# Two attention stages of a decoder kernel: the order of Norm's transposes, the second scores and the turned value products

## The chip, the cores and the metric

The kernel runs on one core of one Trainium2 chip. The metric is the device time of one launch in microseconds (us). The kernel before takes 1344.28 us, the median of 3 runs (1343.42 to 1345.02).

## The reference

A decoder of two layers over 32 sequences of 128 tokens with 256 features. Each layer adds three blocks to x, each on a LayerNorm of x:

```python
x = x + _L0_attn_ref(_layernorm(x), ...)         # 16 heads of 16, rotary factors on q and k
x = x + _L0_xattn_ref(_layernorm(x), ctx, ...)   # entangled cross attention, one head
x = x + _L0_ffn_ref(_layernorm(x), ...)          # routed experts with low-rank parts
x = x + _L1_attn_ref(_layernorm(x), ...)         # 16 heads of 16
x = x + _L1_xattn_ref(_layernorm(x), ctx, ctx, mask, ...)   # 16 heads, one mask row for all
x = x + _L1_ffn_ref(_layernorm(x), ...)          # ternary weights, inner LayerNorm
# a head: softmax(q k^T / 4) v; then the output projection
```

## The kernel before

The residual x stays in SBUF. Work goes by groups of two sequences (256 tokens), 16 groups a layer. `attention_stage` runs twice: once for the first block ("the first stage" below, with rotary factors, `rope`), and once for the fourth and fifth blocks together ("the second stage": 16 self groups, then 16 cross groups with a mask, `at(G)[0].cross`). Between them and behind them lie stages that the change doesn't touch.

Each engine has its own program, a function `group(G, parity)` made of `first_half` and `second_half`; the engines meet only through semaphores, so the order in which each function issues its steps is the order on that engine. A group G overlaps with three others: its Norm and projections are made while G-1 and G-2 are in their attention. Groups 3 to 10 of a layer are in a hardware loop, the others are unrolled, and the unrolled ones also carry pieces of preparing the next stage's weights.

For one sequence of a group (half a group) the steps are these.

- `maximum_scores` (TensorE, L1307): a cheap pass of q k^T, "first scores", in tiles of 32 rows, four heads' strips at a time, in four PSUM banks. It waits until the exponentials of three of the four banks of the sequence before are done. VectorE takes the row maxima, `max_step` (L1093), four times.
- `scores` (L1316): the exact "second scores", three passes, again in tiles of 32 rows, into the S2 banks, three of which are those of the first scores. It waits for the first three maxima.
- `turn_maxima` (L1358): one matmul turns the 16 maxima of each row into rows; ScalarE copies them, `take_rows` (L886); `shift_scores` (L1368) subtracts them from the scores with 16 small matmuls in tiles of 32 rows ("the strips"). In cross groups GpSimd makes the shifts (`shift_step`, L825, four a sequence) and `shift_scores` adds them with full tiles (L1377).
- `exp_step` (ScalarE, L875), four a sequence; then `weighted_values` (L1389, tiles of 32 columns) into the bank AV.
- `raw_heads` (ScalarE, L880) copies AV, `turn` (TensorE, L1396) transposes it ("value products' turn"), `normalise` (VectorE, L1099 and L1102) divides by the sums, `turn_back` (L1402) transposes back, `out_high` and `out_low` split the result, and `output` projects it.

For the next groups: `transposes(G + 2)` (TensorE, L217) turns the normalised x ("Norm's turns"), `act_high` (ScalarE, L223) and `dve_low` (VectorE, L227) split it in two parts, and `queries`, `keys` and `values` project it, three passes each (all L105). ScalarE and VectorE then make masked and split copies: `masked_q` (L911) and `low_q` (L1137) for each of two head masks, `high_k` (L918 with rope, L924 without, L921 with a bias), `low_k` (VectorE L1158, in the first stage GpSimd L833). `values` waits for `low_k` where there is no rope.

In `first_half` of TensorE the order before is: Norm's turns of G + 2, second scores of G, turn of the maxima, turn of the value products of G-1's second sequence, strips, values of G + 1. In that of ScalarE: `raw_heads`, `act_high`, `masked_q` (or `high_k`), `take_rows`, four exponentials. `fill` issues matmuls on a tile of ones, whose result is not used; L142. At G = -1 of the first stage no group is in attention: TensorE turns the Norm of group 1 and projects the values of group 0 and the queries of group 1. Before group 0 TensorE and VectorE add a value bias (`value_bias`).

## Time and profile before

| what | value |
|---|---|
| median of 3 runs | 1344.28 us |
| the profiled execution's own time | 1346.47 us |
| its span | 1344.7 us |
| TensorE busy (PE) | 1278.7 us, 95% of the span |
| VectorE busy (DVE) | 995.6 us, 74% |
| ScalarE busy (ACT) | 847.5 us, 63% |
| GpSimd busy (POOL) | 468.7 us, 35% |
| mean granted TensorE clock | 0.984 |

A row of the timeline gives start, busy time, engine, line, operation, output<-input, shapes, and how many instructions are merged in it; in brackets the idle time of the engine before it and who ended it. A merged row's busy time runs to the end of its last instruction, and an instruction of TensorE is shown busy until its result has left the array, while the next one of the same kind may start earlier. So the step from start to start of two rows is what counts on TensorE's path.

### The profile page before, as it was taken

To read this page: it belongs to the slowest core of one execution; us is meant where nothing else is said; L and a number is where in the kernel's file an instruction comes from. 1 tells how busy PE (TensorE), PEld (TensorE's weight loads), DVE (VectorE), ACT (ScalarE), POOL (GpSimd) and SP (SyncE) were. 2 spreads that over 40 slices of the span, in tenths; PEclk is the share of its full clock that TensorE was granted. 3 is DMA by queue.
4 is the path that set the end of the run, shared out by engine and by line. 5 is a ranking of instruction groups with operands and counts; after the bars stand their busy time and mean duration, and the time that the engine had idled before them with its cause. 6 is when DMAs were issued, how large, how long until landed. Compare 5 with 4: busy or idle time off the path is not lost. (4 is left out here: it accounts for less than half of the span.)

```text
span 1344.7 us, 40781 instructions
## 1 busy us (share of the span) xinstructions
PE 1278.7 (95%) x15088; PEld 1124.8 (84%) x15088; DVE 995.6 (74%) x2421; ACT 847.5 (63%) x1723; POOL 468.7 (35%) x578
## 2 busy tenths in 40 slices
PE   8999999799989999999899999999999999799997
PEld 7788888689979999998788888788888877589987
DVE  6788888556655555563898888788888888568886
ACT  4788887455555455453677777676666676356563
POOL 2223222032221212120100000056666657478884
PEclk9999999999988999999999999999999999899999
DMA  7000000031110000001010000000000000000000
GB/s 241 2 3 0 0 1 2 2 125 39 32 33 1 1 0 0 0 2 51 7 65 1 0 0 2 10 17 18 18 16 16 16 10 2 17 9 31 23 32 32
DMA packets 17189, 29.57 MB, mean 22 GB/s; under 512 B 3920, under 2 KB 8016, under 8 KB 16688
## 3 DMA queue, kind: packets, MB, share of 16 engines
q1 hardware_dynamic: 17072, 27.98, 6.3%
q8 instruction: 77, 1.26, 0.4%
q14 instruction: 40, 0.33, 0.1%
HBM read 23.78 MB, written 4.19 MB: 21 GB/s over the span
## 5 line engine op out<-in xcount | busy, mean ns | idle before, releaser
L875 ACT ACTIVATE a_probs<-a_S 128x512 f32<-128x512 f32 x384 | 200.8, 604 | 50.5 <-PE a_S L1377 31.2
L186 POOL TENSOR_TENSOR all_var_eps<-all_moments,all_ln_eps 128x2 f32<-128x2 f32 x96 | 24.3, 253 | 533.6 <-DVE all_moments L181 521.3
L1093 DVE TENSOR_REDUCE a_row_max<-a_S 128x4 bf16<-128x512 f32 x256 | 164.2, 682 | 19.8 <-PE a_S L1307 19.6
L825 POOL TENSOR_TENSOR a_shifts<-a_add_mask,a_cross_max 128x512 bf16<-128x512 bf16 x128 | 143.3, 1140 | 78.9 <-DVE a_cross_max L1093 78.9
L1389 PE MATMUL a_AV<-a_probs,a_v_pad 128*32 128x128 f32 x3072 | 104.2, 276 | 6.8 <-issue 3.0
L880 ACT ACTIVATE a_av_raw<-a_AV 128x512 f32<-128x512 f32 x96 | 57.5, 599 | 71.0 <-PE a_AV L1389 70.9
L1389 PEld LDWEIGHTS a_AV<-a_probs,a_v_pad 128*32 128x32 f32 x3072 | 78.6, 110 | 20.7 <-issue 4.3
L105 PE MATMUL c_OUT<-all_odd_split,c_h_hi 128*128 128x256 f32 x512 | 94.9, 283 | 0.9 <-DVE all_x_res L2065 0.9
L1316 PE MATMUL a_S<-a_qm_hi,all_odd_split 32*128 32x256 f32 x1536 | 94.1, 302 | 0.3
L1137 DVE SCALAR_TENSOR_TENSOR a_qm_lo<-a_q,all_head_mask,a_qm_hi 128x512 fp32r<-128x512 f32 x96 | 87.3, 911 | 0.2 <-ACT a_qm_hi L911 0.2
L1093 DVE TENSOR_REDUCE a_cross_max<-a_S 128x4 f32<-128x512 f32 x128 | 82.6, 682 | 4.1 <-PE a_S L1339 3.4
L2187 POOL TENSOR_TENSOR d_scaled_hid<-d_hid,all_odd_weights 128x512 f32<-128x512 f32 x64 | 81.5, 1293 | 9.6 <-ACT d_hid L2219 8.4
L209 DVE TENSOR_SCALAR all_xn<-all_x_res,all_moments,all_rstd 128x256 f32<-128x256 f32 (+1 forms) x136 | 72.7, 576 | 15.4 <-POOL all_rstd L188 14.6
L1316 PEld LDWEIGHTS a_S<-a_qm_hi,all_odd_split 32*128 32x128 f32 x1536 | 66.8, 183 | 18.6 <-issue 10.2
L105 PEld LDWEIGHTS c_OUT<-all_odd_split,c_h_hi 128*128 128x128 f32 x512 | 79.7, 189 | 1.0 <-issue 1.0
L178 DVE BATCH_NORM_STATS2 all_stats<-all_x_res 128x6 f32<-128x256 f32 (+1 forms) x192 | 71.5, 414 | 5.5 <-DMA all_x_res<-in_x 2.4
L891 ACT ACTIVATE all_odd_split<-a_AV 128x256 fp32r<-128x256 f32 x96 | 36.7, 382 | 57.9 <-PE a_AV L1402 57.9
L2049 DVE TENSOR_TENSOR c_h_lo<-c_h,c_h_hi 128x512 fp32r<-128x512 f32 x64 | 45.8, 716 | 36.6 <-ACT c_h_hi L2029 36.6
L2023 ACT ACTIVATE c_h<-c_HB,all_odd_weights 128x256 f32<-128x256 f32 x128 | 53.8, 471 | 29.0 <-PE c_HB L2096 28.1
L105 PE MATMUL c_OUT<-all_odd_split,c_h_lo 128*128 128x256 f32 x256 | 71.8, 281 | 0.0
L833 POOL TENSOR_TENSOR all_odd_split<-a_k,all_odd_split 128x512 fp32r<-128x512 f32 x16 | 20.7, 1292 | 146.2 <-ACT all_odd_split L918 146.2
L188 POOL TENSOR_TENSOR all_rstd<-all_var_eps,all_minus_half 128x2 f32<-128x2 f32 x96 | 67.2, 700 | 7.5
(309 smaller groups left out, 3971.6 us busy)
## 6 DMA issues: line engine op xcount, KB each, us to landing
all_cx<-in_ctx_turned SPq DMA_DIRECT2D x16, 256.0 KB, 2.6
all_cx<-in_ctx SPq DMA_DIRECT2D x16, 256.0 KB, 2.6
out_x<-all_x_res SPq DMA_DIRECT2D x16, 256.0 KB, 2.0
all_x_res<-in_x SPq DMA_DIRECT2D x7, 512.0 KB, 8.8
b_routed_wi<-in_L_ffn_wi_W SPq DMA_DIRECT2D x1, 1024.0 KB, 5.1
b_routed_wo<-in_L_ffn_wo_W SPq DMA_DIRECT2D x1, 1024.0 KB, 7.0
all_even_weights<-in_L_ffn_W_fc SPq DMA_DIRECT2D x1, 1024.0 KB, 4.9
all_even_weights<-in_L_ffn_W_proj SPq DMA_DIRECT2D x1, 1024.0 KB, 6.9
```

Of the source, the lines that this page charges most:

```text
L105: last = pe.matmul(out, w(k), m(k), start=(begins and k == 0 and n == 0), stop=(ends and k == chunks - 1 and n == 2))
L178: dve.bn_stats(self.stats[:, b, :], self.x(w, b)).then_inc(self.link, 1)
L188: pool.tensor_tensor(self.rstd[:], self.var_eps[:], self.minus_half[:], ALU.pow).then_inc(self.rstd_ok, 1)
L209: last = dve.tensor_scalar(self.xn[:, b, :], self.x(w, b), self.moments[:, b, 0:1], self.rstd[:, b:b + 1], ALU.subtract, ALU.mult)
L825: pool.tensor_tensor(shifts[:, j], add_mask[:], cross_max[:, j, :].rearrange("p (h o) -> p h o", o=1).to_broadcast([P, QH, P]), ALU.subtra ...
L875: act.activation(probs[:, b * NQ + j, :], S2[j][:], ACT.Exp, scale=DH ** -0.5).then_inc(exp_ok, 1)
L880: act.activation(av_raw[:], AV[:], ACT.Copy).then_inc(raw_ok, 1)
L1093: dve.tensor_reduce((cross_max if at(G)[0].cross else row_max)[:, j, 0:QH], S1[j][:].rearrange("p (h k) -> p h k", h=QH), AXX, ALU.max).th ...
L1137: dve.scalar_tensor_tensor(qm_lo[par][:, :, :, v, :], by_seq(q32), head_mask[:, v:v + 1], f32(qm_hi[par][:, :, :, v, :]), op0=ALU.mult, op ...
L1316: pe.matmul(S2[j][:, c * HV * P:(c + 1) * HV * P], k[par][strip, c, tok], q[par][strip, c, b].rearrange("p h t -> p (h t)"), start=(c == 0 ...
L1389: last = pe.matmul(AV[32 * h:32 * h + 32, j * P:(j + 1) * P], v_pad[par][:, b, j * QH + h, :], probs[:, b * NQ + j, h * P:(h + 1) * P], st ...
L2187: pool.tensor_tensor(half_of(scaled_hid[parity], n), half_of(hid[parity], n), gain_row[:, half * HB_COLS:(half + 1) * HB_COLS], ALU.mult). ...
```

## The change

It moves steps in both halves of the engines' programs and adds fill matmuls at one place.

- TensorE, `first_half`: second scores and the turn of the maxima come first; behind them Norm's turns; then the strips; then, in self groups, the turn of the value products. In cross groups that turn stays ahead: scores, turn of the value products, Norm's turns, shifts.
- ScalarE, `first_half`: `act_high` of Norm goes behind `masked_q`/`high_k` and `take_rows`, directly ahead of the exponentials.
- ScalarE, `second_half` at G = -1 of the first stage: normalising group 2 goes ahead of the masked queries of group 1.
- VectorE, `first_half` with rope: the second `low_q` follows the first, ahead of `normalise` (not at G = -1).
- TensorE at G = -1 of the first stage: 5 fill matmuls ahead of the values of group 0, where there were none. The second stage keeps its 3.

```diff
@@ scalar, first_half
                     raw_heads((G - 1) * PAIR + 1)
+                piece(G, 0)
+                if inside(G + 1):
+                    if rope:
+                        masked_q(G + 1, odd, 1)
+                    else:
+                        high_k(G + 1, odd)
+                if inside(G) and not at(G)[0].cross:
+                    take_rows(G, 0)
                 if normed_here(G + 2):
                     lay, n = at(G + 2)
                     lay.norm.act_high(act, n, FA, lay.xT_hi[parity])
...
                     next_norm.act_high(act, 0, FA)
-                piece(G, 0)
-                if inside(G + 1):
-                    if rope:
-                        masked_q(G + 1, odd, 1)
-                    else:
-                        high_k(G + 1, odd)
-                if inside(G) and not at(G)[0].cross:
-                    take_rows(G, 0)
@@ scalar, second_half
+                if x_dram is not None and at_first(G, -1):
+                    first.norm.act_normalise(act, 2)
                 if inside(G + 2):
                     masked_q(G + 2, parity, 0)
@@ vector, first_half
                         low_q(G + 1, odd, 0)
+                        if not at_first(G, -1):
+                            low_q(G + 1, odd, 1)
...
                     normalise((G - 1) * PAIR + 1)
                 piece(G, 1)
-                if rope and inside(G + 1):
+                if rope and at_first(G, -1):
                     low_q(G + 1, odd, 1)
@@ tensor, first_half
+                made = inside(G) and at(G)[0].cross
+                if inside(G):
+                    scores(G, 0, parity)
+                    if not made:
+                        turn_maxima(G, 0)
+                if made and inside(G - 1):
+                    turn((G - 1) * PAIR + 1)
+                piece(G, 0)
                 if normed_here(G + 2):
                     transposes(G + 2)
                 if last_of(G):
                     next_transposes()
                 if inside(G):
-                    scores(G, 0, parity)
-                    if not at(G)[0].cross:
-                        turn_maxima(G, 0)
-                if inside(G - 1):
+                    shift_scores(G, 0)
+                if not made and inside(G - 1):
                     turn((G - 1) * PAIR + 1)
-                piece(G, 0)
-                if inside(G):
-                    shift_scores(G, 0)
                 piece(G, 1)
-                if x_dram is None and at_first(G, -1):
-                    fill(pe, consts, S2[0], 3)
+                if at_first(G, -1):
+                    fill(pe, consts, S2[0], 5 if x_dram is not None else 3)
                 if inside(G + 1):
                     values(G + 1, odd)
```

## Rows read from the trace of the kernel before

**Rows 1.** The page, part 1: busy time, share of the span, instructions.
```profile
PE 1278.7 (95%) x15088; PEld 1124.8 (84%) x15088; DVE 995.6 (74%) x2421; ACT 847.5 (63%) x1723; POOL 468.7 (35%) x578
```

**Rows 2.** Timeline of one first half in the first stage's loop, group 9.
```profile
157.17 1.88 DVE L1093 TENSOR_REDUCE a_row_max<-a_S 128x4 bf16<-128x512 f32 x3
...
157.69 1.08 PE L1389 MATMUL a_AV<-a_probs,a_v_pad 128*32 128x128 f32 x32
...
158.70 0.66 PE L217 MATMUL a_FA<-all_ident,all_xn 128*128 128x128 f32 x4
...
158.83 0.60 ACT L880 ACTIVATE a_av_raw<-a_AV 128x512 f32<-128x512 f32 x1 [0.44 <-PE a_AV L1389]
...
159.28 0.39 PE L1316 MATMUL a_S<-a_qm_hi,all_odd_split 32*128 32x256 f32 x4
...
159.88 0.71 ACT L911 ACTIVATE a_qm_hi<-a_q,all_head_mask 128x512 fp32r<-128x512 f32 x1
...
160.19 0.23 PE L1358 MATMUL a_S<-all_ident_b,a_row_max 128*128 128x128 bf16 x1
...
160.26 0.61 PE L1396 MATMUL a_AV<-all_ident,a_av_raw 128*128 128x128 f32 x4
...
160.54 0.28 ACT L886 ACTIVATE a_max_rows<-a_S 128x128 bf16<-128x128 f32 x1
...
160.87 0.40 PE L1368 MATMUL a_S<-a_max_rows,all_minus_rows_b 32*128 32x128 bf16 x16
...
161.20 0.39 PE L105 MATMUL a_FB<-all_odd_split,all_xT_hi 128*128 128x256 f32 x1
...
161.38 2.06 ACT L875 ACTIVATE a_probs<-a_S 128x512 f32<-128x512 f32 x4 [0.56 <-PE a_S L1368]
...
161.61 0.74 DVE L1137 SCALAR_TENSOR_TENSOR a_qm_lo<-a_q,all_head_mask,a_qm_hi 128x512 fp32r<-128x512 f32 x1
...
163.01 0.51 PE L1307 MATMUL a_S<-a_km,a_q_hi 32*128 32x256 f32 x8
...
163.63 0.69 DVE L1093 TENSOR_REDUCE a_row_max<-a_S 128x4 bf16<-128x512 f32 x1 [0.68 <-PE a_S L1307]
```

**Rows 3.** The same timeline, value products followed directly by second scores.
```profile
165.24 1.08 PE L1389 MATMUL a_AV<-a_probs,a_v_pad 128*32 128x128 f32 x32
...
166.25 0.39 PE L1316 MATMUL a_S<-a_qm_hi,all_odd_split 32*128 32x256 f32 x4
```

**Rows 4.** Timeline of the second stage, self groups in the loop.
```profile
747.62 1.08 PE L1389 MATMUL a_AV<-a_probs,a_v_pad 128*32 128x128 f32 x32
...
750.45 0.69 DVE L1158 TENSOR_TENSOR all_odd_split<-a_FB,all_odd_split 128x512 fp32r<-128x512 f32 x1 [0.75 <-ACT all_odd_split L924]
...
752.95 0.39 PE L1307 MATMUL a_S<-a_km,a_q_hi 32*128 32x256 f32 x4
```

**Rows 5.** Timeline of the second stage, a self group behind the loop.
```profile
820.41 1.08 PE L1389 MATMUL a_AV<-a_probs,a_v_pad 128*32 128x128 f32 x32
...
825.60 0.51 PE L1307 MATMUL a_S<-a_km,a_q_hi 32*128 32x256 f32 x8
```

**Rows 6.** Timeline of the second stage, a cross group.
```profile
1006.67 3.48 POOL L825 TENSOR_TENSOR a_shifts<-a_add_mask,a_cross_max 128x512 bf16<-128x512 bf16 x3 [0.48 <-DVE a_cross_max L1093]
...
1010.42 1.68 PE L105 MATMUL a_FB<-all_odd_split 128*128 128x256 f32 x12
...
1012.03 0.51 PE L1307 MATMUL a_S<-a_km,a_q_hi 32*128 32x256 f32 x8
```

**Rows 7.** Timeline of the first stage's start, groups -1 and 0.
```profile
17.57 0.36 PE L105 MATMUL a_FB<-all_odd_split,all_xT_hi 128*128 128x256 f32 x1 [1.35 <-DVE all_odd_split L309]
...
27.25 0.63 PE L217 MATMUL a_FA<-all_ident,all_xn 128*128 128x128 f32 x4 [1.24 <-ACT all_xn L201]
...
29.16 1.49 DVE L1137 SCALAR_TENSOR_TENSOR a_qm_lo<-a_q,all_head_mask,a_qm_hi 128x512 fp32r<-128x512 f32 x1 [0.16 <-ACT a_qm_hi L911]
```

**Rows 8.** Busy times by stretch, the start; PEclk is granted clock.
```profile
18.00:22.00 4.00, 4.00 (x23) 3.87 (x21) 2.25 (x8) 2.32 (x4) 1.20 (x1) 0.57 1.02 416
```

More of the change, by code:

```diff
@@ L1028, in second_half @@
                         masked_q(G + 2, parity, 1)
-                if x_dram is not None and inside(G + 3) and not at_first(G, -2):
+                if x_dram is not None and inside(G + 3) and not at_first(G, -2) and not at_first(G, -1):
                     first.norm.act_normalise(act, G + 3)
```

## The prediction, made before the changed kernel was run

> **What bounds the kernel now.** I read the page first: TensorE is busy 95% of the span, VectorE 74%, ScalarE 63%, GpSimd 35% [rows 1]. So time comes back only where TensorE's path gets shorter, and the reader should distrust the busy share: TensorE's busy time holds the tail of each last result, in which nothing new enters. I therefore went to the timeline of one first half and read only starts on TensorE [rows 2]. From value products (157.69) to the next first scores (163.01) it goes: +1.01 Norm's turns, +1.59 second scores, +2.50 turn of the maxima, +2.57 value products' turn, +3.18 strips, +3.51 values, +5.32 first scores. Three places are no work. Norm's turns sit between two tiled kinds of matmuls and take 0.58 to the next start, though four turns need only 0.45: a turn step is (0.61 - 0.27) / 3 = 0.11 in the row of the value products' turn, where I take 0.27 as the length of one. The strips wait for ScalarE's copy of the rows. And the first scores wait for the third exponential: exponentials start at 161.38, three take 1.55 (three quarters of 2.06), the first scores start 0.08 behind them. The second half of a group has no moved step.
>
> **The change, part by part, in a first half of a self group.** Time runs from the start of the value products' matmuls.
>
> Second scores directly behind value products: +1.01, which the other half of the same group shows [rows 3], instead of +1.59. They need three of the four maxima; the last three run from 157.17 for 1.88, so the third of the four is done at 157.17 + 2 x 0.63 = 158.43, and 157.69 + 1.01 = 158.70 is 0.27 behind it: the data are there. Turn of the maxima at +1.01 + 0.91 = +1.92 (0.91 is 160.19 - 159.28 [rows 2]). Norm's turns issue behind it, +1.98 to +2.43, and fill the gap that the value products' turn filled.
>
> The rows' copy. ScalarE does raw heads (start +1.14), 0.60, then masked queries, 0.71 less 0.05 of overlap, then the rows: start +2.35, where it was +2.85, because Norm's copy no longer lies ahead. TensorE alone would allow +1.92 + 0.35 = +2.27, so ScalarE is late by 0.08. Strips 0.33 behind the rows' start: +2.68. Then 0.33 (strips to the next full tile), value products' turn 0.45, values at +3.46 instead of +3.51. So of 0.5 us by which the rows come earlier, nearly all is spent again on the turn that now lies between strips and values.
>
> First scores. Norm's copy (0.60) follows the rows: its data are ready at +1.98 + 0.61, it ends near +3.2, and the exponentials start at +3.2 instead of +3.69. The third is done at +4.8, so it no longer decides. Values to first scores, not held by an exponential, take 1.61 in a cross group [rows 6]. That gives +5.07, against +5.32: **0.25 us a group** in groups 1 to 10 of the first stage, 2.5 us.
>
> VectorE in that half: both low queries, then normalise, then Norm's low part. Its next maxima waited 0.68 us for the first scores [rows 2]. The turned value products come 0.45 later, which delays normalise by as much; the second low query, 0.74, no longer follows it. The sum ends about where the new first scores want it. But GpSimd adds its bias (L819) in group after group near that place, just behind the first low query; one such instruction beside GpSimd took 1.49 instead of 0.74 [rows 7]. Of the slack of 0.68, 0.25 goes to the first scores that come earlier, and 0.43 is left. From below the price is 0 (the low query keeps its 0.74), from above (the whole 0.75 more) 0.75 - 0.43 = 0.32 a group, which would eat the gain. I take 0, since the nearest row, the slack of this very half, covers most of it. In groups 11 to 13 of this stage VectorE has moments of the next stage's Norm in the half and no such slack, so I count 0.05 each, 0.15. Group 14 has no Norm's turns: the value products' turn leaves a gap it had filled and lies on the path, +0.35. Group 15 has no values; there the exponentials decide alone and start earlier, -0.35.
>
> Second stage, self groups. Before, +5.33 [rows 4]: values wait for the low part of k (750.45 + 0.69 = 751.14), which waits for ScalarE's high part behind Norm's copy. Now the high part is done 0.5 earlier. ScalarE: 1.15 + 0.60 + 0.59 - 0.05, so rows at +2.29, strips +2.62, values +3.40, first scores +5.01: 0.32 a group in the 8 groups of the loop, 2.6 us. Unrolled groups take +5.19 before [rows 5]: 0.18, six of them, 1.1 us. Groups 0 and 15 I count at 0; they wait for other things. Together 3.65 us.
>
> Cross groups. The last of GpSimd's three shifts ends at 1006.67 + 3.48 = 1010.15, and values start 0.27 behind [rows 6], the time of the four matmuls that need it and a wait. TensorE gets there earlier now and waits longer: 0. ScalarE's exponentials start some 0.1 later (Norm's copy lies ahead of them), but the first scores there are set by the values. Bounds over 16 groups: +0.1 each, if the exponentials decide, and -0.13 each, if the saved gap counts. I take 0.
>
> The start of the first stage. TensorE stood 1.24 us for the normalised x of group 2 [rows 7] and only then did second scores of group 0. Now the scores go first, and that normalising goes ahead of the masked queries. The next limit is VectorE: value bias, fourth maximum, scaled key, two low queries (the second 1.49), Norm's low part, which queries of group 2 need. It moves little, so of 1.24 I keep 0.7. The fills: the granted clock is 0.57 between 18 and 22 us [rows 8], that is mostly at the lower of its two levels (1.2 of 2.4 GHz), after TensorE had stood 1.35 us [rows 7]. Five fills cut that idle time by 5 x 0.11. If the clock then stays up, the work of these 4.00 busy us takes 4.00 x 0.57 = 2.3: 1.7 less, some of which goes into the wait for the low part of group 1's Norm, which comes no sooner. Bounds 0 and 1.7; I take 1.2, since an idle time of 1.24 at 27.25 was followed by no fall. Start together 1.9.
>
> The Trainium skill (TensorE: Matmul & The Clock Gate, "What's actually happening") says that the chip's watch on activity runs free and isn't restarted by a kernel. By that rule the same fills could miss in one execution and help in the next; the sum would then be 7.0 in some and 8.2 in others. The trace before has one execution and can't say.
>
> The Trainium skill (TensorEngine Tiling (Array Packing), "Key Properties") says that a change of tiling mode drains TensorE. By that rule alone the change removes one such change a group, 0.13 by my reading, 3.8 us over 29 self groups; the rows give more because two waits go with it.
>
> Sum: 2.5 + 0.15 - 0.35 + 0.35 + 3.65 + 0 + 1.9 = **8.2 us**. The profiled execution took 1346.47 (span 1344.7), 2.2 above the median of the runs; from it, 1338.3; from the median of 1344.28, 1336.1. I forecast **1336.5 us**, 0.4 being left for what groups 0 and 15 may lose.
>
> **Rivals.**
> - *Clock not lifted, small gains halved by late signals.* Terms are differences of 0.05 to 0.3 us. With the start at 0.7 and the per-group gains at half: 0.7 + 1.3 + 1.8 = 3.8, so 1340.5. For it: ScalarE is already 0.08 late for the rows. Against: the starts repeat to 0.05 from group to group.
> - *VectorE takes over in the first stage.* The second low query at 1.49 plus the later turn hold Norm's low part and the maxima: the first stage gives nothing. Only the second stage pays, 3.65, less 0.1 for each of 16 cross groups: 2.05, so 1342.2. GpSimd's place speaks for it, the 0.68 of slack against it.
> - *Slower.* Both low queries stretch to 1.49 beside GpSimd in the first stage. Then Norm's low part ends 1.5 later than before, 0.68 of it in the slack: +0.8 in 13 groups, +10.4, less 3.65 of the second stage and 0.7 at the start, plus 0.1 for each of 16 cross groups: +7.7, so 1352. The whole turns slower once these 13 groups lose over (3.65 + 0.7) / 13 = 0.33 each, that is when that part ends over 1.0 later than before. Against it: the first low query lies at its old place, beside small GpSimd work only.
> - *More.* A later fall of the clock in the first groups also goes (another 1.7), cross groups give 0.13 each (2): 1332.5.
>
> **How the numbers follow.** Forecast 0.55, half gains 0.2, VectorE in the first stage 0.1, slower 0.05, more 0.1. A measurement of this kernel can tell about 0.2%, 2.7 us, from no change. Forecast, more, and most of the half gains lie beyond it: faster 0.82; same 0.13 (VectorE's case and a part of the half gains); slower 0.05. The range is 1331 to 1342: it holds forecast, half gains and the more case, and leaves VectorE's and the slower case out, with the edges of the forecast.
>
> **What would show it.** In the first stage's loop the distance from the start of value products to the first scores falls from 5.32 to about 5.07, with second scores at +1.01, rows at +2.35 and exponentials at +3.2; in the second stage's from 5.33 to 5.01. Cross groups keep their distances, with a longer wait for the last shift. The granted clock between 18 and 22 us is 1.0. The second low query stays at 0.74, or takes 1.49 with the maxima late behind it. The prediction is wrong if the low part of Norm ends behind the first scores by over 0.6 us, or if cross groups get longer.

## The result and the profile after

The changed kernel takes 1334.07 us (median of 6 runs, 1330.1 to 1335.49), the kernel before 1344.65 beside it on the same chip (6 runs): 10.6 us less, a ratio of 0.9917, interval 0.9902 to 0.9931. The forecast was 1336.5. The profiled execution took 1334.29, span 1332.4. Three executions, two of the changed kernel and one of the kernel before, took 1528 to 2732 us and are left out of every comparison below.

First the page of the changed kernel: its part 1, which answers to [rows 1], and the exponentials' row of part 5.

```profile
PE 1268.8 (95%) x15098; PEld 1123.8 (84%) x15098; DVE 993.8 (75%) x2421; ACT 843.9 (63%) x1723; POOL 477.2 (36%) x578
...
L875 ACT ACTIVATE a_probs<-a_S 128x512 f32<-128x512 f32 x384 | 200.5, 609 | 27.0 <-PE a_S L1381 24.4
```

The page of the kernel before had the same exponentials with almost twice the idle time ahead of them:

```profile
L875 ACT ACTIVATE a_probs<-a_S 128x512 f32<-128x512 f32 x384 | 200.8, 604 | 50.5 <-PE a_S L1377 31.2
```

The busy shares say nothing (TensorE 95% both times). What is left ahead of the exponentials is the wait for the masked shifts of cross groups (L1381); the wait for the strips has gone.

Next the timeline of the changed kernel, the first half of a group of the first stage's loop, in the columns of [rows 2].

```profile
110.85 1.08 PE L1393 MATMUL a_AV<-a_probs,a_v_pad 128*32 128x128 f32 x32
...
111.86 0.39 PE L1320 MATMUL a_S<-a_qm_hi,all_odd_split 32*128 32x256 f32 x4
...
112.78 0.23 PE L1362 MATMUL a_S<-all_ident_b,a_row_max 128*128 128x128 bf16 x1
...
112.84 0.61 PE L217 MATMUL a_FA<-all_ident,all_xn 128*128 128x128 f32 x4
112.88 2.24 DVE L1139 SCALAR_TENSOR_TENSOR a_qm_lo<-a_q,all_head_mask,a_qm_hi 128x512 fp32r<-128x512 f32 x2
112.95 1.62 POOL L819 TENSOR_TENSOR all_x_res<-all_x_res,all_odd_weights 128x512 f32 x1
113.12 0.28 ACT L886 ACTIVATE a_max_rows<-a_S 128x128 bf16<-128x128 f32 x1
...
113.45 0.40 PE L1372 MATMUL a_S<-a_max_rows,all_minus_rows_b 32*128 32x128 bf16 x16
113.49 0.60 ACT L223 ACTIVATE all_xT_hi<-a_FA 128x512 fp32r<-128x512 f32 x1
...
113.79 0.66 PE L1400 MATMUL a_AV<-all_ident,a_av_raw 128*128 128x128 f32 x4
...
113.98 2.06 ACT L875 ACTIVATE a_probs<-a_S 128x512 f32<-128x512 f32 x4
...
114.20 0.36 PE L105 MATMUL a_FB<-all_odd_split,a_xT_hi_odd 128*128 128x256 f32 x1
...
115.73 0.68 DVE L227 TENSOR_TENSOR all_xT_lo<-a_FA,all_xT_hi 128x512 fp32r<-128x512 f32 x1
115.78 0.51 PE L1311 MATMUL a_S<-a_km,a_q_hi 32*128 32x256 f32 x8
...
116.40 0.69 DVE L1095 TENSOR_REDUCE a_row_max<-a_S 128x4 bf16<-128x512 f32 x1
```

From value products' start (110.85) to the next first scores it is now 4.93, where [rows 2] have 5.32. The third exponential ends at 113.98 + 1.55 = 115.53; the first scores start 0.25 later, so values decide them, no longer an exponential.

Not every group gets this. The next rows of the changed kernel's timeline are a group that follows the jump back in the loop (two groups per pass), and then the same group in the kernel with early waits (below):

```profile
96.47 1.08 PE L1393 MATMUL a_AV<-a_probs,a_v_pad 128*32 128x128 f32 x32
...
97.74 0.39 PE L1320 MATMUL a_S<-a_qm_hi,all_odd_split 32*128 32x256 f32 x4 [0.19 <-issue]
...
101.67 0.51 PE L1311 MATMUL a_S<-a_km,a_q_hi 32*128 32x256 f32 x8
```

Second scores start at +1.27 there, not +1.01, behind idle time that nothing in the profile releases ("issue"), and the first scores at +5.20. It is so in the first group of every pass of the loops but the first pass: +1.27, +1.19, +1.18 in the first stage, +1.31, +1.24, +1.19 in the second.

Where the time went, by distances between first scores. The last column is a second profiled execution of the changed kernel. In brackets: how many us of the stretch lie at the lower level of the granted clock (1.2 of 2.4 GHz), where there are any.

| stretch | before | changed | changed, again |
|---|---|---|---|
| start, to the first scores of group 2 | 54.1 (6.8) | 52.0 (3.4) | 50.1 |
| first stage, groups 2 to 15 | 194.1 | 191.2 | 191.3 |
| between the stages, with the second stage's group -1 | 392.0 (20.5) | 389.1 (13.7) | 391.1 (20.5) |
| second stage, groups 0 to 2 | 46.8 (3.4) | 49.3 (10.2) | 48.1 (6.8) |
| groups 3 to 13 | 160.1 | 157.2 | 157.2 |
| groups 14, 15 and the step to cross groups | 35.2 (3.4) | 34.4 (3.4) | 33.6 |
| cross groups | 270.6 | 269.5 | 269.3 |
| behind them (untouched) | 191.6 (8.5) | 189.8 (5.1) | 189.8 (5.2) |

The last stretch has no edit and still differs by 1.8 us; it has 3.4 us less at the lower level. Falls of the granted clock are 3.4 to 10.2 us long here, and their number differs between executions of one kernel. The stretch between the stages holds one edited place, the second stage's group -1, where ScalarE now makes k's high part ahead of Norm's copy. TensorE's values of group 0 wait there for k's low part, in the kernel before and in the changed one:

```profile
637.24 0.38 PE L105 MATMUL a_FB<-all_even_split,all_xT_hi 128*128 128x256 f32 x1 [1.28 <-DVE all_odd_split L1158]
```
```profile
629.22 0.39 PE L105 MATMUL a_FB<-all_even_split,all_xT_hi 128*128 128x256 f32 x1 [0.79 <-DVE all_odd_split L1160]
```

That is 0.5 us of the 2.9 (it comes with TensorE's old order too), and the rest goes with 6.8 us less at the lower level. So I read two more things than the median. Over 49 runs of the kernel before, the time follows the mean granted clock by 1.0 us per 0.001 (correlation -0.90; clocks 0.982 to 0.990, times 1340.3 to 1349.4). Below, "at equal clock" is the mean distance of a kernel's runs from that line, with its standard error; the clock is given to three places, and the line's slope is that of one kernel, so it is a reading and no second measurement. The changed kernel stands at -9.9 (0.35), its repetition at -9.8 (0.6).

### The profile page after: what moved, and what is told of

Its sections match the earlier page's. It is cut to its first block and busy times, and to the rows that moved or that the text cites. A ratio compares the mean times of both kernels' runs of the same rounds, so it can differ in the third digit from the quotient of the medians.

```text
span 1332.4 us, 40789 instructions
## 1 busy us (share of the span) xinstructions
PE 1268.8 (95%) x15098; PEld 1123.8 (84%) x15098; DVE 993.8 (75%) x2421; ACT 843.9 (63%) x1723; POOL 477.2 (36%) x578
```

## The experiments

All times are medians beside the kernel before on the same chip; ratios are to it. The diffs are shortened: several steps may stand on one line.

**One of the two engines' orders put back.** With ScalarE's order as before:

```diff
@@ scalar, first_half (changed kernel)
-                piece(G, 0); masked_q / high_k; take_rows(G, 0)
                 Norm's act_high; next_norm.act_high
+                piece(G, 0); masked_q / high_k; take_rows(G, 0)
```

> The changed kernel with ScalarE's order in the first half undone (Norm's copy ahead of masked queries and the rows' copy), TensorE's new order kept. Theory: the two orders belong together. Norm's turns end 2.6 us behind the start of value products, so Norm's copy holds the rows' copy until about +3.9 (it is +2.27 in the changed kernel) and first scores come at about +6.5 instead of +4.93 in the loop of the first stage; over 29 self groups 40 us or more slower than the changed kernel, near 1375 us. Rival: TensorE's order alone brings the gain, and first scores stay within 0.2 of +4.93, total 1334 to 1340 us.

1399.04 us (4 runs), ratio 1.0389 (1.0371 to 1.0406): 53 us slower than the kernel before, 65 slower than the changed one. The timeline of this kernel, in the first stage's loop:

```profile
120.86 1.08 PE L1393 MATMUL a_AV<-a_probs,a_v_pad 128*32 128x128 f32 x32
...
122.85 0.61 PE L217 MATMUL a_FA<-all_ident,all_xn 128*128 128x128 f32 x4
123.49 0.60 ACT L223 ACTIVATE all_xT_hi<-a_FA 128x512 fp32r<-128x512 f32 x1 [0.89 <-PE a_FA L217]
...
124.60 0.27 ACT L886 ACTIVATE a_max_rows<-a_S 128x128 bf16<-128x128 f32 x1
...
124.92 0.40 PE L1372 MATMUL a_S<-a_max_rows,all_minus_rows_b 32*128 32x128 bf16 x16 [1.47 <-ACT a_max_rows L886]
...
127.25 0.51 PE L1311 MATMUL a_S<-a_km,a_q_hi 32*128 32x256 f32 x8
```

ScalarE waits 0.89 for Norm's turns, which TensorE now issues behind the second scores, and only then serves the queries and the rows: rows at +3.74, first scores at +6.39. I had not thought of the cross groups, which in this execution are 19 us longer than in the changed kernel (288.6 against 269.5).

With TensorE's order in self groups as before and ScalarE's as changed:

```diff
@@ tensor, first_half, self groups (changed kernel)
+                transposes(G + 2); next_transposes()
                 scores(G, 0, parity); turn_maxima(G, 0)
-                transposes(G + 2); next_transposes()
-                shift_scores(G, 0); turn(...)
+                turn(...); shift_scores(G, 0)
```

> TensorE's order in self groups as before (Norm's turns ahead of the second scores, value products' turn ahead of the strips), everything else as changed: ScalarE takes Norm's copy behind the rows, VectorE's low queries together, the start's edits. My theory: ScalarE's order alone gives nothing in the loop, since the rows' copy then waits for TensorE's turn of the maxima (+2.51 behind the value products, rows at +2.86 as before, exponentials at +3.7 with Norm's copy ahead of them) and first scores stay at +5.3; only the start's 2 us come: about 1342, the first half 7.5 us long. The rival: part of the gain is ScalarE's, because k's high part no longer waits behind Norm's copy; then the second stage's loop falls by 0.1 to 0.3 us a group, about 1339. If Norm's copy, now behind the rows, makes the exponentials late instead, the loop gets longer by up to 0.2 us a group: about 1345.

1341.22 us (10 runs), ratio 0.9973 (0.996 to 0.9986); at equal clock -1.7 (0.25). Its timeline:

```profile
113.19 0.23 PE L1362 MATMUL a_S<-all_ident_b,a_row_max 128*128 128x128 bf16 x1
...
113.54 0.28 ACT L886 ACTIVATE a_max_rows<-a_S 128x128 bf16<-128x128 f32 x1 [0.50 <-PE a_S L1362]
...
116.01 0.51 PE L1311 MATMUL a_S<-a_km,a_q_hi 32*128 32x256 f32 x8
```

The group's value products start at 110.68 here, so the first scores are at +5.33 and the rows at +2.86, to 0.01 where they were before. ScalarE was ready but waited 0.50 for TensorE's turn of the maxima. In the second stage's loop it is +5.33 too, although k's high part no longer waits behind Norm's copy: the forecast's reason for a larger gain there (k's chain) does not hold the loop by itself. So in self groups ScalarE's order alone gives nothing, TensorE's alone costs 53 us, and both together give 8 of the 10 us.

**The start's edits alone**, on the kernel before (5 fills; group 2's normalising ahead of the masked queries):

```diff
@@ tensor, first_half (kernel before)
-                if x_dram is None and at_first(G, -1):
-                    fill(pe, consts, S2[0], 3)
+                if at_first(G, -1):
+                    fill(pe, consts, S2[0], 5 if x_dram is not None else 3)
@@ scalar, second_half
+                if x_dram is not None and at_first(G, -1):
+                    first.norm.act_normalise(act, 2)
```

> The kernel before with only the two edits of the first stage's start: 5 fill matmuls ahead of the values of group 0 and the normalising of group 2 ahead of the masked queries of group 1; all orders as before. Theory: the fills do not decide the clock (without them it stayed up in one execution of the changed kernel as well) and the early normalising takes most of the 1.24 us wait at 27 us: group 0's second scores come 0.8 to 1.2 us earlier than before, total 1344 us; the rest of the start's gain needs the new order. Rival: the start's edits alone bring its full 2.2 us, 1343 us, with full clock from 18 to 22 us. And if the falls of the clock at 638 to 655 us appear here too, they do not come from the new order.

1342.35 us (10 runs), ratio 0.9986 (0.9972 to 1.0); at equal clock -1.3 (0.26). In its profile the start takes 52.1 us to group 2's first scores, beside 54.1 and 52.0, and the rest is as before (194.1, 160.1, 270.2). Of its 2.0 us, 1.1 lie between the first scores of group 0's two sequences (9.24 before, 8.10 here), where the wait of 1.24 was [rows 7]. That is these edits' gain, and it agrees with the 1.3 at equal clock. The other 1.0 lies ahead of group 0's first scores (22.2 before, 21.1 here), where the kernel before had the fall of [rows 8].

**The fills.** The changed kernel without them:

```diff
@@ tensor, first_half (changed kernel)
-                if at_first(G, -1):
-                    fill(pe, consts, S2[0], 5 if x_dram is not None else 3)
+                if x_dram is None and at_first(G, -1):
+                    fill(pe, consts, S2[0], 3)
```

> The changed kernel without the 5 fill matmuls at the first stage's start. Theory: the fills keep the granted clock up between 18 and 22 us; without them it falls as before and first scores of group 0 start at 22.2 us instead of 21.2, with the first full group 1.0 to 1.3 us later than in the changed kernel; total about 1335.2 us. Rival: the fall went for another reason (the later work or the phase of the chip's watch), the clock stays at full level there and the total is 1334 us.

1334.43 us (4 runs), ratio 0.9909 (0.9887 to 0.9931), as with them. The timeline and the window from 18 to 22 us without fills, the latter in the columns of [rows 8]:

```profile
17.64 0.36 PE L105 MATMUL a_FB<-all_odd_split,all_xT_hi 128*128 128x256 f32 x1 [1.36 <-DVE all_odd_split L309]
...
18.00:22.00 4.00, 3.82 (x35) 3.34 (x35) 2.69 (x9) 1.77 (x4) 1.44 (x2) 1.00 1.02 409
```

TensorE stood 1.36 us, as before the change (1.35), and the clock stayed at its upper level. With fills it was 1.00 too. Group 0's first scores start at 21.1 us without fills and at 20.8 to 21.2 us in all other traces but that of the kernel before. So the fills are not what keeps the clock up; that the fall of [rows 8] belonged to that one execution is not shown directly, since the kernel before has one trace. More fills, at group 0 of each stage (8 ahead of the second scores, in the second stage only, 8 behind them, 14 ahead of the next first scores):

```diff
@@ tensor, first_half (changed kernel)
+                if at_first(G, 0):
+                    pe.wait_ge(q_taken, 2)
+                    if x_dram is None: fill(pe, consts, FA, 8)
                 scores(G, 0, parity)
+                if at_first(G, 0): fill(pe, consts, FA, 8)
@@ tensor, second_half
+                if at_first(G, 0):
+                    pe.wait_ge(v_free, 2)
+                    fill(pe, consts, FB, 14)
```

> The changed kernel with fill matmuls in the idle times of group 0: in the second stage 8 ahead of the second scores, in both stages 8 behind them and 14 ahead of the next group's first scores (0.11 us each at full clock). Theory: the falls of the granted clock that follow these idle times (at 37 us, and at 638 and 651 us, 13.6 us of lower clock together) go or halve, 1.7 us less for each 3.4 us at the lower level where TensorE is the bound: 3 to 5 us faster than the changed kernel, 1330 us. Rival: the falls come anyway, or the fills delay the work behind them by as much as they save: 1333 to 1336 us.

1335.48 us (4 runs), ratio 0.9925 (0.9899 to 0.9951). The clock did rise, to 0.990 to 0.994, and the falls in group 1 of both stages went. Windows over the first fall, of the changed kernel, then of this one:

```profile
34.00:44.00 10.00, 8.14 (x126) 6.88 (x125) 6.97 (x17) 7.73 (x16) 4.15 (x6) 0.83 0.01 2
```
```profile
34.00:44.00 10.00, 10.00 (x165) 8.57 (x157) 6.57 (x17) 7.43 (x17) 3.56 (x6) 1.00 0.01 2
```

Group 1's first half falls from 8.65 to 7.09 us, but group 0's two halves grow from 8.32 and 6.79 to 9.41 and 8.18: 2.5 paid for 1.6 in the first stage.

**VectorE's second low query put back** behind the normalising:

```diff
@@ vector, first_half (changed kernel)
-                        if not at_first(G, -1):
-                            low_q(G + 1, odd, 1)
...
-                if rope and at_first(G, -1):
+                if rope and inside(G + 1):
                     low_q(G + 1, odd, 1)
```

> The changed kernel with VectorE's order undone: the second low query goes behind normalise again. Theory: the value products' turn is now late, so the low query and Norm's low part run one behind the other after it; Norm's low part starts at about +5.0 instead of +4.34 to +4.88, queries and maxima of the first stage wait for it, 0.1 to 0.2 us a group in 13 groups, 1.3 to 2.5 us slower than the changed kernel. Rival: the slack of this half covers it, distances unchanged within 0.03 us, total the same as the changed kernel, 1334 us.

1334.58 us (4 runs), ratio 0.9914 (0.9898 to 0.9931), not told apart from the changed kernel; at equal clock -6.5 (0.27). Its timeline:

```profile
113.47 0.74 DVE L1139 SCALAR_TENSOR_TENSOR a_qm_lo<-a_q,all_head_mask,a_qm_hi 128x512 fp32r<-128x512 f32 x1
113.55 1.61 POOL L819 TENSOR_TENSOR all_x_res<-all_x_res,all_odd_weights 128x512 f32 x1
115.78 0.74 DVE L1139 SCALAR_TENSOR_TENSOR a_qm_lo<-a_q,all_head_mask,a_qm_hi 128x512 fp32r<-128x512 f32 x1
...
116.44 0.68 DVE L227 TENSOR_TENSOR all_xT_lo<-a_FA,all_xT_hi 128x512 fp32r<-128x512 f32 x1
```

Value products start at 111.45. The first scores stay at +4.93, but Norm's low part starts at +4.99 instead of +4.88 (in the groups between +5.2 instead of +4.5 to +4.6), and the next value products come at +7.34 instead of +7.19. The first stage is 1.7 us longer (192.95). The edit shortens the chain to the queries, not to the scores. The line gives 3.4 us; the rest beyond 1.7 I can't place, so the line can be wrong by over 1 us.

**The value products' turn ahead of Norm's turns and strips:**

```diff
@@ tensor, first_half (changed kernel)
-                if made and inside(G - 1):
+                if inside(G - 1):
                     turn((G - 1) * PAIR + 1)
                 piece(G, 0)
...
                     shift_scores(G, 0)
-                if not made and inside(G - 1):
-                    turn((G - 1) * PAIR + 1)
```

> The changed kernel with the value products' turn ahead of Norm's turns and the strips in self groups too (as in cross groups). TensorE's own sum hardly changes. Theory: what the place behind the strips buys is the exponentials: with the turn first, Norm's turns end 0.45 us later, Norm's copy on ScalarE ends at about +3.7 instead of +3.2 and the exponentials start there instead of +3.13; the first scores come at about +5.3 instead of +4.93 in the loop, so nearly the whole gain of a self group goes: 0.35 us in some 29 groups, 10 us, total near 1343 us. Rival: only TensorE's count of mode changes and gaps matters; first scores within 0.1 of +4.93 and the total 1334 to 1336 us.

1340.86 us (10 runs), ratio 0.9977 (0.9965 to 0.999); at equal clock -2.2 (0.28): most of the gain is gone. Its timeline, value products at 112.03:

```profile
114.47 0.60 PE L217 MATMUL a_FA<-all_ident,all_xn 128*128 128x128 f32 x4
...
115.11 0.60 ACT L223 ACTIVATE all_xT_hi<-a_FA 128x512 fp32r<-128x512 f32 x1 [0.52 <-PE a_FA L217]
...
115.60 2.06 ACT L875 ACTIVATE a_probs<-a_S 128x512 f32<-128x512 f32 x4
...
117.22 0.51 PE L1311 MATMUL a_S<-a_km,a_q_hi 32*128 32x256 f32 x8 [0.21 <-ACT a_probs L875]
```

Norm's turns come 0.45 later, ScalarE waits 0.52 for them, the exponentials start at +3.57 instead of +3.13, and the third decides the first scores again, at +5.19. Where the turn goes is worth 0.26 a group. Over whole stages nothing is left of the self groups' gain: groups 2 to 15 of the first stage take 194.5 us and groups 3 to 13 of the second 160.0, against 194.1 and 160.1 in the kernel before. So the third piece of the change, the turn behind the strips, is as needed as the two orders.

**Cross groups as before**, TensorE's and ScalarE's orders:

```diff
@@ tensor and scalar, first_half (changed kernel), where at(G)[0].cross
+                transposes(G + 2); next_transposes()   (ahead of scores)
+                Norm's act_high                        (ahead of piece(G, 0))
```

> The changed kernel with the cross groups' old order on TensorE and ScalarE (Norm's turns ahead of second scores, Norm's copy first), self groups as changed. Theory: the cross groups gain 0.10 us each by their new order (8.68 to 8.78 between the first scores of the two sequences), so this one is 1.0 to 1.6 us slower than the changed kernel, 1335.3 us. Rival, as predicted at first: GpSimd's shifts set these groups and their order is worth nothing; distances 8.68 and total 1334 us.

1333.42 us (4 runs), ratio 0.9903 (0.9887 to 0.992), not told apart. In the trace the cross groups take 270.8 instead of 269.5, the first halves of the first ten groups 8.67 to 8.79 instead of 8.59 to 8.68. Timeline of this kernel, then of the changed one:

```profile
979.90 1.08 PE L1400 MATMUL a_AV<-a_probs,a_v_pad 128*32 128x128 f32 x32
981.50 0.39 PE L1327 MATMUL a_S<-a_qm_hi,all_odd_split 32*128 32x256 f32 x4
...
985.63 0.51 PE L1318 MATMUL a_S<-a_km,a_q_hi 32*128 32x256 f32 x8
```
```profile
979.38 1.08 PE L1393 MATMUL a_AV<-a_probs,a_v_pad 128*32 128x128 f32 x32
980.39 0.39 PE L1320 MATMUL a_S<-a_qm_hi,all_odd_split 32*128 32x256 f32 x4
...
985.00 0.51 PE L1311 MATMUL a_S<-a_km,a_q_hi 32*128 32x256 f32 x8
```

The second scores come 0.59 earlier. The pair above shows 5.73 against 5.62, but in groups 4 to 10 that difference isn't the order's: the start's edits alone, with the old order, have 5.63 in most of these groups, and the changed kernel without fills, with the new order, has 5.73 in most. What repeats in every trace (but that with ScalarE's order put back): groups 0 to 3 go from 5.61-5.63 to 5.54, the first half of group 11 falls by 0.56 and that of group 12 by 0.33, and that of group 15 grows by 0.50. The cross groups take 270.2 to 270.8 us in the three traces with the old order and 269.3 to 269.5 in the two of the changed kernel.

**The register waits early.** The second scores' waits for queries and keys, whose values depend on the loop's counter, go ahead of the second half's last value products:

```diff
@@ tensor (changed kernel)
+            def ready_to_score(G):
+                pe.wait_ge(qmhi_ok, ...); pe.wait_ge(qmlo_ok, ...); pe.wait_ge(khi_ok, G + 1)
+                if not rope: pe.wait_ge(klo_ok, G + 1)
@@ scores, b == 0
-                    pe.wait_ge(qmhi_ok, ...) and the other three
+                    if is_first(G): ready_to_score(G)
+                    if rope: pe.wait_ge(klo_ok, G + 1)
@@ second_half
+                if inside(G) and inside(G + 1): ready_to_score(G + 1)
                 weighted_values(G, 1, parity)
```

> The changed kernel with three or four of the waits of the first second scores of a group issued ahead of the value products before them; the waits for maxima and exponentials stay. In the changed kernel each pass of the hardware loop but the first starts its second scores at +1.19 to +1.31 instead of +1.01. Theory: that is TensorE's sequencer working off the waits behind the loop's branch, no longer hidden behind Norm's turns; with fewer waits there it falls to about +1.05, 0.15 to 0.3 us in 3 groups of each of three layers, 1 to 2 us faster than the changed kernel, 1332.5 us. Rival: it is the branch itself (or fetching the loop's code), and the starts stay at +1.19 to +1.31, total 1334 us.

1331.89 us (4 runs), ratio 0.9912 (0.9887 to 0.9937); at equal clock -11.6 (0.4). Its timeline:

```profile
96.34 1.08 PE L1401 MATMUL a_AV<-a_probs,a_v_pad 128*32 128x128 f32 x32
97.35 0.39 PE L1320 MATMUL a_S<-a_qm_hi,all_odd_split 32*128 32x256 f32 x4
...
101.23 0.51 PE L1311 MATMUL a_S<-a_km,a_q_hi 32*128 32x256 f32 x8
```

Second scores at +1.01 and first scores at +4.89 in the group that stood behind the loop's jump, and so in all six (first scores at +4.95 in the second stage). It takes the jump and the waits together: the loop's other groups have the same waits and start at +1.01 in the changed kernel too, and here the jump is still there. Whether it matters that the waits' values come from the loop's counter, and not only how many waits there are, is not shown. This kernel and the changed one were measured again, beside each other:

> The changed kernel itself once more, for comparison on the same chip in the same rounds: ratio to the kernel before 0.992 as it was (0.990 to 0.994). It also tells how much of a second profiled execution's stage lengths is the clock: my theory is that the distances of groups at full clock repeat within 0.02 us and that the start of the second stage (49.3 us where other executions of near kernels have 46.9 to 48.1) does not repeat; the rival is that it belongs to the changed order and repeats at 49.3.

> The changed kernel with the register-valued waits early, once more, beside the changed kernel in the same rounds. My theory: some 1.3 us faster than the changed kernel, from the distances of the loop-back groups (7.08 instead of 7.30 us) and of the second stage's loop: 1332.5 where the changed kernel has 1334. The rival: no difference, because the waits only move idle time of TensorE to where the scalar engine ends the wait anyway.

The changed kernel: 1332.94 (4 runs), ratio 0.9927 (0.9899 to 0.9955). Early waits: 1331.39 (6 runs), ratio 0.9918 (0.9891 to 0.9944). Ten runs of each together: 1331.7 against 1333.4 in the mean, ratio 0.9987, interval 0.9973 to 1.0001. The traces repeat (first stage 190.5 and 190.3 against 191.2 and 191.3; groups 3 to 13 of the second 156.5 and 156.4 against 157.2 twice), so the distances show 1.5 us, and the times nearly, but not quite, tell them apart. Of the second expectation half fell: the second stage's start did come back at 48.1.

The best of all, with early waits, no fills, and the value products' turn ahead of the strips where no Norm's turns lie (group 14):

```diff
@@ tensor, first_half (kernel with early waits, without the 5 fills)
+                norms = normed_here(G + 2) or last_of(G)
+                if not made and not norms and inside(G - 1): turn(...)
                 shift_scores(G, 0)
-                if not made and inside(G - 1): turn(...)
+                if not made and norms and inside(G - 1): turn(...)
```

> The changed kernel with three edits: the register-valued waits of the second scores moved ahead of the values of the group before (as in the run with early waits), the five fills ahead of the first group's second half left out, and the turn of the value products ahead of the strips in the groups without Norm's turns (group 14 of each stage). My theory: the early waits give 0.2 us in each of the 6 loop-back groups of the first two stages and about 0.1 in every other loop group, some 1.5 us; the fills give nothing; group 14 returns from +4.90 to about +4.65 behind the value products, 0.25 us in each of two stages. Sum about 2 us: ratio to the kernel before about 0.990, and 0.998 to the changed kernel. The rival: the clock's falls, whose number differs by several us of low clock from execution to execution, cover all of this, and no difference to the changed kernel beside it can be told; group 14 must show +4.65 all the same.

1332.7 us (6 runs), ratio 0.9923 (0.9902 to 0.9943); at equal clock -12.3 (0.23), the lowest. All its runs fell at clocks of 0.985 to 0.987. Its timeline of group 14:

```profile
223.22 1.08 PE L1401 MATMUL a_AV<-a_probs,a_v_pad 128*32 128x128 f32 x32
...
227.85 0.50 PE L1311 MATMUL a_S<-a_km,a_q_hi 32*128 32x256 f32 x8
```

+4.63, where the changed kernel has +4.90. The second stage's group 14 has Norm's turns (of the first cross groups) and stays at +4.86, so the expectation's second 0.25 us had no ground. Against the ten runs of the changed kernel its ratio is 0.9995 (0.9989 to 1.0003). So neither variant is shown to beat the changed kernel in time, though both have shorter distances.

## Why the prediction was right, and where not

**The first stage: the mechanism right, the sum close because misses cancel.** Second scores +1.01 as forecast, exponentials +3.13 (+3.2), first scores +4.93 (+5.07). The rows come at +2.27, not +2.35 (the forecast's own terms, 1.14 + 0.60 + 0.71 - 0.05, add to 2.40): ScalarE is not late, the two copies overlap by more; the turn takes 0.41 instead of 0.45, values to first scores 1.58 instead of 1.61. What I missed with the other sign: three groups in a stage, those behind the loop's jump, start at +1.2 to +1.3. In [rows 2] Norm's turns lay directly behind the value products and the second scores came later, so that these waits cost nothing; with the scores first they are on the path. Groups 2 to 15 gained 2.9 us; my terms, with group 1, say 2.65. By parts: the first halves of groups 2 to 10 gained 2.85 (forecast 2.25), those of groups 11 to 13 0.86 (forecast 0.15, since I gave them no slack), those of 14 and 15 lost 0.2 (forecast 0), and the second halves, which I took to have no moved step and so no change, lost 0.6, most of it in groups 10, 13 and 14.

**Low queries beside GpSimd: the stretch came, and VectorE absorbed it.** Two took 2.24 in the half shown: the first, begun 0.08 ahead of GpSimd's bias, kept its 0.74, and the second, begun 0.58 behind the bias's start, took 1.58. In the next group the bias starts 0.1 behind the second one, and both keep 0.74. Norm's low part ends at 116.41 and the maximum follows at once, 0.62 behind the first scores' start, as in [rows 2]. The whole slack of 0.68 is eaten and nothing more. That I took 0 of a possible 0.32 came out by a hair. By its letter this meets a sign that the prediction named for being wrong: Norm's low part ends 0.63 behind the first scores' start, and it said over 0.6. The maxima are not later for it than in [rows 2], so the limit was drawn a little too low.

**Group 14 lost 0.26** (forecast 0.35); **group 15 did not gain 0.35 but 0.05.** Its second scores start at +1.39, and the row names VectorE's maxima: the last three begin at 237.92, 0.14 ahead of the value products (238.06), so the third of four is done only at about +1.1. In the loop they begin 0.5 ahead [rows 2]. With early waits the second scores start at +1.01, but that is no gain: the value products themselves start 0.35 later behind the maxima, and from first scores to first scores the half takes 6.92 instead of 6.94.

**Second stage: the sum right, its reason wrong.** Loop groups +5.33 to +4.93 and, behind the loop, +5.19 to +4.86, more than 0.32 and 0.18, with +5.14 to +5.25 in the three behind the jump. Groups 2 and 3 (3 is the loop's first) gave nothing (first halves 7.41 to 7.40 and 7.55 to 7.54). The changed kernel's timeline in group 2, value products at 668.82:

```profile
669.67 0.69 DVE L309 TENSOR_TENSOR all_odd_split<-all_even_weights,all_odd_split 128x512 fp32r<-128x512 f32 x1
...
671.02 0.23 PE L1362 MATMUL a_S<-all_ident_b,a_row_max 128*128 128x128 bf16 x1 [0.21 <-DVE a_row_max L1095]
```

VectorE splits weights between the third and the fourth maximum; the fourth ends at 670.96, and the turn of the maxima waits for it. So it is in group 3. All in all 2.9 in groups 3 to 13, 0.3 in group 14 and 0.3 in group 1 (7.42 to 7.09 where no fall of the clock lies in it): 3.5 against 3.65. The rest of the 0.9 at the end lies in the step to the cross groups, which holds a fall in both kernels; without a fall the new order and TensorE's old one have the same step, 11.1 and 8.0 us. The run with TensorE's old order shows that k's chain alone had not held the +5.33. Where it did hold TensorE, in group -1 of this stage, the sum had no term, and 0.5 us came.

**Cross groups: 1.2 us, forecast 0**, within the bounds (-0.13 a group). The forecast let the values stand behind the last shift; 0.09 a group of TensorE's earlier time arrives in groups 0 to 3, and groups 11 and 12 give 0.9 and group 15 takes 0.5 back. That is 0.7 to 0.8 us that repeats; the rest of the 1.2 lies in groups 4 to 10, which differ by as much between traces of one order. The sign "if cross groups get longer" did not come for the stage as a whole.

**Start: 2.2 us, forecast 1.9, and half of it luck.** First scores of group 0 come 1.0 earlier (21.2 against 22.2). I gave 1.2 to a clock kept up by fills; the fills do nothing, and the clock stays up without them, so as far as these traces can tell this 1.0 is the difference between two executions and not the change. The rest is the change: the wait of 1.24 for group 2's Norm is gone [rows 7], 0.9 in group 0's first half (forecast 0.7), and group 1's first half gives 0.3, together 1.2. The forecast's 1.0 for the clock between 18 and 22 us came true for a wrong reason. The Trainium skill (TensorE: Matmul & The Clock Gate, "What's actually happening") says that the watch runs free of the kernel; that falls come and go between two executions of the changed kernel agrees with it.

**A term that the sum had not: the clock in the second stage's start.** The first half of group 1 took 7.42 us in the profiled executions of the kernel before, of the start's edits alone and of the turn first, whose fall of 3.4 us lies in group 0's first half. In both of the changed kernel it took 8.6, because a fall of 3.4 us lies in it, and without a fall (more fills) 7.09: 0.33 gained became 1.2 lost. Both of the changed kernel have another fall in group 0 as well. The three groups take 46.8 us with 3.4 us at the lower level (before), 46.9 with 3.4 (early waits), 48.1 with 6.8 and 49.3 with 10.2 (changed). The changed kernel's window there, in the columns of [rows 8]:

```profile
650.00:656.00 6.00, 5.63 (x78) 4.91 (x78) 4.05 (x10) 2.92 (x7) 0.89 (x2) 0.72 0.01 3
```

It isn't the new order alone: with TensorE's old order the half had its fall too, 8.91 us. What sets the place of this fall stays open. In the first stage the same idle time of TensorE, 1.86 us ahead of group 1's first scores, was followed by a fall in one execution of the changed kernel and by none in the other.

Terms against traces, away from the clock's falls: 2.65, 3.65, 0 and 1.9 forecast; 2.9, 3.5, 1.2 and 1.2 measured, and 0.5 in the second stage's group -1, for which there was no term: 9.3 in place of 8.2. The runs at equal clock say 9.9 (0.35). So the total came this near to the forecast partly by luck: the fills' 1.2 brought nothing, and the cross groups (0.7 to 1.2) and group -1 (0.5), forecast at nothing, made up for it.

## What to carry to other kernels

When a step moves on one engine, move its consumer on the next engine too: here one order alone gave nothing, the other alone cost 53 us, both together gained 8, and with one further step left at its old place that gain was gone. Ask of a gain read from two traces how much of it is the clock of either: here 1.0 of the start's 2.2 us was. Read a predicted distance in both groups of a loop pass: the one behind the jump has waits that earlier work hid. With a clock whose falls differ between executions, judge edits of 1 or 2 us by distances that repeat to 0.02 us, and the total by many runs.

## What the runs showed of the hardware

- A fall of the granted clock of 3.4 us, over a half that is otherwise 7.05 to 7.09 us long, made it 8.65: 1.6 us. Two executions of the changed kernel differ in this at 37 us.
- Waits against values of the loop's counter, issued right behind a loop's jump, hold TensorE 0.17 to 0.30 us. The same waits in a group not behind the jump, or issued ahead of the 1 us of value products in front of it, cost nothing.
- VectorE's low query takes 0.74 by itself, and also when GpSimd's bias (1.62 us) starts 0.08 behind it. Begun 0.58 behind the bias's start, it took 1.58.
